# An attention and mixture-of-experts kernel: the transposition of each expert's next rows moved from TensorE to four DMA transposes

## The reference

```
xn    = x / rms(x) * norm_weight                 # 8192 x 512
idx   = top 512 tokens of each expert, by logit  # 16 x 512
h     = gelu(xn[idx] @ fc1[e].T + fc1_bias)      # 512 x 2048
y     = h @ fc2[e].T + fc2_bias                  # 512 x 512
out   = x + sum over experts of gate * y / sum of the token's chosen gates
```

## Time and profile before

| | us |
|---|---|
| median of 3 runs | 1980.07 (1979.4 to 1982.03) |
| the profiled execution | 1975.57 |
| its span in the trace | 1973.9 |
| TensorE matmul busy | 1897.5 (96%) |
| VectorE busy | 1493.6 (76%) |
| ScalarE busy | 1307.7 (66%) |
| GpSimd busy | 1224.7 (62%) |
| mean granted TensorE clock | 0.994 of full speed |

### The profile page before, as it was taken

How to read it: one execution, slowest core, us unless ns; L and a number is a source line. 1 busy time by engine, 2 the same in 40 slices (tenths; PEclk the granted TensorE clock), 3 DMA queues, 4 the chain that set the end, 5 groups by cost and what they waited for, 6 DMA issues and landing times.

```text
span 1973.9 us, 42032 instructions
## 1 busy us (share of the span) xinstructions
PE 1897.5 (96%) x12637; PEld 1693.8 (86%) x12637; DVE 1493.6 (76%) x2360; ACT 1307.7 (66%) x2594; POOL 1224.7 (62%) x1230
## 2 busy tenths in 40 slices
PE   4889999998889999999999999999999999999998
PEld 3678888877778899999998989899999999989897
DVE  5778878776887878777787777777787878778764
ACT  4667777763456666767677676767667676766664
POOL 3578888874056747566475756657574757657461
PEclk9999999999999999999999999999999999999999
DMA  7664444435743525254343534344352525335352
GB/s 283 219 193 151 120 132 135 120 87 182 238 107 114 148 94 154 86 152 107 125 121 122 142 104 135 101 138 127 113 153 87 155 86 154 107 128 133 112 123 44
DMA packets 90258, 263.19 MB, mean 133 GB/s; under 512 B 20593, under 2 KB 22353, under 8 KB 85073
## 3 DMA queue, kind: packets, MB, share of 16 engines
q1 hardware_dynamic: 70866, 211.44, 33.4%
q0 software_dynamic: 17024, 34.19, 8.9%
q10 hardware_dynamic: 2304, 16.78, 2.3%
HBM read 223.47 MB, written 55.60 MB: 141 GB/s over the span
## 4 chain that ended last, share of the span: by engine, by line
PE 71%; DVE 3%; issue 1%; POOL 0%; ACT 0%; DMA 0%; DVEq 0%; ACTq 0%; POOLq 0%
PE experts_b_a L2342 18%; PE experts_b_y L259 12%; PE experts_b_y L260 12%; PE experts_b_y L261 12%; PE experts_b_b L2342 9%; PE experts_b_c L2342 5%; PE experts_b_turn L2312 1%; PE experts_b_a L2442 1%; PE experts_b_c L2331 1%; PE experts_b_turn L2331 1%; DVE experts_y_out L2126 1%; DVE experts_x_lo L1987 0%; DVE experts_counts L2138 0%; DVE experts_hot_a L1911 0%; DMA experts_rows<-xn_dram,experts_ahead 0%
## 5 line engine op out<-in xcount | busy, mean ns | idle before, releaser
L1606 POOL TENSOR_TENSOR experts_s_raw<-experts_w_raw 128x256 f32<-128x256 f32 x128 | 156.4, 1222 | 406.7 <-DMA experts_w_raw<-in_w 392.3
L259 PE MATMUL experts_b_y<-experts_w_hi,experts_h_hi 128*128 128x512 f32 x1024 | 406.4, 397 | 1.2 <-DVE experts_h_lo L2065 1.2
L260 PE MATMUL experts_b_y<-experts_w_lo,experts_h_hi 128*128 128x512 f32 x1024 | 404.2, 395 | 0.0
L261 PE MATMUL experts_b_y<-experts_w_hi,experts_h_lo 128*128 128x512 f32 x1024 | 399.3, 390 | 0.0
L2342 PE MATMUL experts_b_a<-experts_x_hi,experts_w_hi 128*128 (+1 forms) x1024 | 288.5, 282 | 1.4 <-ACT experts_h L1814 0.7
L2342 PE MATMUL experts_b_a<-experts_x_hi,experts_w_lo 128*128 (+1 forms) x1024 | 289.6, 283 | 0.0
L2342 PE MATMUL experts_b_a<-experts_x_lo,experts_w_hi 128*128 (+1 forms) x1024 | 289.4, 283 | 0.0
L261 PEld LDWEIGHTS experts_b_y<-experts_w_hi,experts_h_lo 128*128 128x128 f32 x1024 | 192.4, 188 | 43.2
L259 PEld LDWEIGHTS experts_b_y<-experts_w_hi,experts_h_hi 128*128 128x128 f32 x1024 | 194.3, 190 | 25.6 <-DVE experts_h_lo L2065 1.6
L260 PEld LDWEIGHTS experts_b_y<-experts_w_lo,experts_h_hi 128*128 128x128 f32 x1024 | 194.3, 190 | 21.2
L2342 PEld LDWEIGHTS experts_b_a<-experts_x_hi,experts_w_hi 128*128 128x128 f32 x1024 | 194.2, 190 | 19.1 <-issue 1.4
(11 more groups left out here) (389 smaller groups left out, 5547.6 us busy)
## 6 DMA issues: line engine op xcount, KB each, us to landing
experts_w_raw<-in_w SPq DMA_DIRECT2D x256, 512.0 KB
bias<-in_bias SPq DMA_DIRECT2D x68, 256.0 KB, 4.1
spread_w<-weight_dram SPq DMA_DIRECT2D x32, 512.0 KB, 6.5
xn_dram<-wq_hi ACTq DMA_DIRECT2D x13, 1024.0 KB, 7.1
attend_q_x<-in_x SPq DMA_DIRECT2D x17, 256.0 KB, 2.8
attend_k_x<-in_x SPq DMA_DIRECT2D x17, 256.0 KB, 6.0
xn_dram<-rows_y_xn SPq DMA_DIRECT2D x17, 256.0 KB, 4.7
experts_b_sb<-in_b SPq DMA_DIRECT2D x16, 256.0 KB
```

What stands on the lines that cost most here:

```text
L259: nc.tensor.matmul(out, lh, rh, start=first, stop=False)
L260: nc.tensor.matmul(out, lh, rl, start=False, stop=False)
L261: return nc.tensor.matmul(out, ll, rh, start=False, stop=last)
L1606: nc.gpsimd.tensor_tensor(s1, a21, a22, ALU.add).then_inc(s_done, 1)
```

## The change

For the experts from the third on (n = 2 to 15, made ready in the 14 turns of the loop), the rows are transposed without TensorE. A float32 value is two 16-bit words. ScalarE copies `rows` into `x_raw` in two instructions, with the low words of a row before its high words (`part_rows`, at the ends of periods 1 and 2). SP waits for both and issues four DMA transposes of 16-bit words, each 128 partitions by 1024 words, from `x_raw` back into `rows` (`move_rows`, ahead of the weight load of its third turn). ScalarE then joins the two words of each value into `x_raw` with four instructions, each of 1024 words a partition (`x_join`), in the places of the former copies; the first waits for all four transposes. TensorE has no transposes and none of their waits in the loop. VectorE's sums read `x_raw` where they read PSUM. The gathers change places: gates at the start of an expert's loop, rows after the tenth chunk's sums of the expert before. `weigh` moves from the middle of period 2 to the end of period 7. The first turn (e = 0) is written out apart from the loop on SP and ScalarE and keeps the transposes on TensorE.

```diff
+                def move_rows(n):
+                    sp.wait_ge(rows_apart, (n - 1) * 2)
+                    alone(sp, passed)
+                    for i, c in enumerate((2, 3, 0, 1)):
+                        sp.dma_start_transpose(moved[:, :, i * P:(i + 1) * P],
+                                               rows_by_word[:, c, :, :].rearrange("p w d -> p (w d)")).then_inc(rows_moved, 16)
+
+                def of_expert(e):
                     for q in range(1, Q + 1):
+                        if q == 3 and not isinstance(e, int):
+                            move_rows(e + 1)
                         if q == 4:
                             load_b2(e)
...
                     alone(pool, passed)
-                        pool.wait_ge(x_turned, n * KD)
+                        if isinstance(n, int) and n == 1:
+                            pool.wait_ge(x_turned, KD)
+                        else:
+                            pool.wait_ge(x_raw_ready, (n - 1) * KD)
...
-                    fetch_rows(e + 1)
                     if first:
+                        fetch_rows(1)
                         weight_sums(2, 5, 1)
                         fetch_meta(1)
                         adopt(0)
+                    else:
+                        fetch_meta(e + 1)
...
                         elif q == 8:
-                            fetch_meta(e + 2)
+                            fetch_rows(e + 2)
...
+                def part_rows(n, a):
+                    half = slice(2 * a, 2 * a + 2)
+                    act.wait_ge(rows_in, n * CT * 16)
+                    nc.scalar.activation(rows_by_word[:, half, :, :], whole_rows[:, half, :, :], ACT.Copy).then_inc(rows_apart, 1)
+
+                def x_join(n, k):
+                    first = RAW_B12 if k < 2 else RAW_B22
+                    act.wait_ge(rows_moved, (n - 1) * CT * 16)
+                    nc.scalar.activation(raw_pairs[:, :, first:first + 2, k % 2, :],
+                                         moved.rearrange("p (w k) (b t) -> p w k b t", k=KD, b=2)[:, :, k, :, :], ACT.Copy)\
+                        .then_inc(x_raw_ready, 1)
...
+                        elif q in (4, 5):
+                            middle = (lambda: x_join(e + 1, (q - 4) * 2),)
+                            end = (lambda: x_join(e + 1, (q - 4) * 2 + 1),)
+                        elif not first and q in (1, 2):
+                            end = (lambda: part_rows(e + 1, q - 1),)
...
-                        elif q in (4, 5):
+                        elif not first and q == 6:
+                            after_c0 = lambda: make_list(e + 2)
+                        elif first and q in (4, 5):
                             after_c0 = lambda: turn_next(e + 1, (q - 4) * 2, e * Q + q)
```

More of the change, by code:

```diff
@@ L45 @@
 EP = E + 2
-CLEARED = 54
+CLEARED = 57
 ATTEND_SIGNALS = {
@@ L1584, in _ @@
                         load_w2(e * Q + (q + 2), q % 2)
+                of_expert(0)
+                with sp.Fori(1, E - 1) as e:
+                    of_expert(e)
                 last = E - 1
@@ L1868, in _, with of_expert @@
                        begin=(lambda: first_split(B22, x_raw[:, RAW_B22, :, :].rearrange("p k t -> p (k t)")), lambda: first_sum_split(T3, 6), lambda: first_sum_split(T4, 8)))
-                with act.Fori(0, E - 1) as e:
-                    side = act.snap((e + 1) % 2)
+                def of_expert(e, side):
+                    first = isinstance(e, int)
                     for q in range(1, Q):
                         middle, end = (), ()
[L1873 to L1878, removed]
+                        if first and q in (4, 5):
+                            middle = (lambda: x_copy(e + 1, (q - 4) * 2, b_c),)
+                            end = (lambda: x_copy(e + 1, (q - 4) * 2 + 1, b_turn),)
+                        elif q in (4, 5):
[3 more added lines that the diff above has]
+                            end = (lambda: part_rows(e + 1, q - 1),)
                         elif q == 6:
@@ L2278, in of_expert @@
                         elif q == 4:
-                            middle = (lambda: x_first(e + 1, 0, b_c),)
-                            end = (lambda: x_first(e + 1, 1, b_turn),)
+                            halves = [b_c[:, 0:HALF], b_turn[:, 0:HALF]] if first else [x_raw[:, RAW_B12, k, :] for k in range(2)]
+                            middle = (lambda: x_first(e + 1, 0, halves[0]),)
+                            end = (lambda: x_first(e + 1, 1, halves[1]),)
                             if first:
@@ L2283, in of_expert @@
                         elif q == 5:
-                            middle = (lambda: x_others(e + 1, 0, b_c),)
-                            end = (lambda: x_others(e + 1, 1, b_turn),)
+                            others = [(b[:, 0:HALF], b[:, HALF:CAP]) for b in (b_c, b_turn)] if first else\
+                                [(x_raw[:, RAW_B22, k, :], x_raw[:, RAW_B21, k, :]) for k in range(2)]
+                            middle = (lambda: x_others(e + 1, 0, *others[0]),)
+                            end = (lambda: x_others(e + 1, 1, *others[1]),)
                         elif q == 6:
@@ L2290, in of_expert @@
                             middle = (lambda: split_x_sums(e + 1, side),)
-                            if first:
-                                end = (lambda: weigh(1),)
+                            end = (lambda: weigh(e + 1),)
                         period(q, e * Q + q, middle=middle, end=end)
@@ L2529, in of_expert @@
                             after_p4 = lambda: turn_next(e + 1, (q - 4) * 2 + 1, e * Q + q)
-                        elif q == 6:
+                        elif first and q == 6:
                             after_c0 = lambda: list_after(e + 2)
```

29 lines of the change are left out of this document (20 added, 9 removed).

## The result

The changed kernel takes 1962.91 us (1957.91 to 1968.33, 5 runs), the one before 1980.45 (1979.4 to 1986.67, 5 runs) beside it: a ratio of 0.9908 [0.9887, 0.9928]. It is faster, by 18 us where 23 were forecast. The profiled execution took 1965.93 us (before 1975.57).

The account below looks back on a forecast made before the run. TensorE's own work was taken to bound the experts. 1975.57 - 24.9 + 1.5 = 1952.2 us for the profiled execution, plus 4.5 for the median, given as 1957; own range 1950 to 1965, wider range 1949 to 2005 at 0.80.

Parts of the forecast that it names:

- Periods 4 and 5: TensorE without transposes: each period falls from 11.44 to 10.55 us, in 14 experts, a gain of 24.9 us.
- ScalarE sorting: Each `part_rows`, after the last split of hidden values: 1.90 us, with ends 0.95 and 3.8; cost 0.
- ScalarE joining: Four copies at 1.05 us replace four of about 0.60; cost 0 if the transposes are there.
- VectorE's narrow place: Period 4, third sum before TensorE's seventh product: spare 0.2 us; loss 0 to 7 us, taken as 1.5.
- SP and the transposes: Issue fits a 4 us gap; landing taken as 9 us against a limit of 15.4 from issue; cost 0.
- GpSimd, "Cost 0": Exchanged gathers: row gathers 1.1 us longer, rows there with 4 us spare, sums 1 us later; cost 0.
- the price of `weigh`: VectorE, end of period 7: five steps under 1.04 us, where VectorE waited 1.02 us.
- The execution's own time: The profiled execution was forecast at 1952.2 us; the median of the runs 4.5 us above, given as 1957.
- 1 and 2: Transposes landing over 15.4 us after issue (0.13), or the queue handling eight blocks per DMA in series, 2369 us (0.11).
- rival 1: Transposes late: ScalarE stops in period 4, TensorE stands before its next period; 2062 us at 22.9 us landing; chance 0.13.
- Rival 4: Part lost at VectorE's narrow place or to 16-bit copies at twice the price: up to 1 us an expert, 1965 to 1976; 0.09.
- Rival 3: Gain given back: transposes take 16 to 18 us, or weights cause the same stall; 1976 to 1984 us; chance 0.07.

Follow-up runs that it names:

- e4_swap_apart: The kernel before with only the exchange of the gathers, and GpSimd's sums waiting for the second `h_lo`: 1977.67 us, ratio 0.9984.
- e1_apart: The changed kernel with GpSimd's four sums held back until VectorE's second `h_lo` of period 0 is done: 1950.74 us, ratio 0.9854.
- e5_turn4: `e1_apart` with the four transposes issued one turn later, at the start of SP's fourth turn: 1958.53 us, ratio 0.9885.
- e6_behind_w1: `e1_apart` with the transposes issued behind the first weight load of SP's fourth turn: 2088.29 us, ratio 1.054.
- after: The changed kernel as first measured, 1962.91 us, ratio 0.9908; its profiled execution took 1965.93 us.
- c_after: The changed kernel run again with no edit: 1962.31 us, ratio 0.9916 against the kernel before.
- e3_swap_only: The kernel before with the gathers exchanged, `weigh` moved and block sums waiting for added rows; TensorE still transposes: 1985.55 us, ratio 1.0042.

## Why the forecast held, and which terms failed

The main term was right by its mechanism. That the sum came within 6 us of the median (1962.9 for 1957) owes something to luck. Its terms add up to 1955.2 with no VectorE loss and to 1962.2 with the whole 7 us; the stated 1950 to 1965 was wider than that without a reason, and the loss that brought the time to its upper end isn't in the sum.

- **Periods 4 and 5, -24.9 us.** Right: 10.55 us each, the expert 85.70 for 87.47, 1.77 us, 14 times. Alone (from `e4_swap_apart` to `e1_apart`) it measures 26 us, with an interval of some 5 us to either side.
- **ScalarE sorting.** Chosen 1.90 us, measured 1.90. Cost 0 is right.
- **ScalarE joining.** Sized at 1.05, measured 1.37: four copies are 5.5 us and not 4.2, and VectorE's sums waited for them 4.5 us in all, 13 times. TensorE stays busy in these periods, so the mis-sizing costs nothing.
- **VectorE's narrow place, +1.5 us.** Nothing there: period 4 is 10.55 in experts where the forecast allowed up to half a microsecond more. The 1.5 us were put at the wrong place on the right engine.
- **SP and the transposes.** The issue takes 5.6 us, longer than the gap of 4 that was read off; the next weight load went at 1036.78, and no split waited for it on TensorE's path. Landing taken as 9 us, measured 7.0 to 7.9 (the join starts 7.5 to 8.7 us after the first issue where it waits, in `e5_turn4`). The limit was put at a join 5.16 us into period 4 (1046.9 less 1041.74); `e5_turn4` shows 5.1, though with a join of 1.37 us and not 1.05: the way from the weights' split to the last gelu was 3.1 us there, where 3.5 were read. "Beyond it every us costs 14" holds just beyond; for a join 7.55 us late the price is 9.5 an expert, a quarter more, for want of the clock in the forecast.
- **GpSimd, "Cost 0". This step failed, and the price of `weigh` with it.** It priced the gathers' lengths and landing, and not what GpSimd's next instructions meet. The sums behind the gather meet the last period's second `h_lo`. Before, with the gates' gather ahead of them, they met it lightly and at no cost; with the rows' gather there they cost 2.0 us in 4 or 5 experts of 15. In the profiled execution it is 10 us; `e1_apart` less the changed kernel gives 11.6 us of the medians. The forecast had seen that "VectorE's phase there depends on what GpSimd does beside it, which moves", and asked it of one place of one period. It priced `weigh` at under 1.04 us too, from its place before, where the five steps take 1.1. At the end of period 7 they take 2.2, beside GpSimd's sums, and VectorE's first sum of the next period starts 2.69 us into it and not 1.64. No run shows what this costs by itself; what follows from it is below. One of the five steps, before and after:

```profile
L1943 DVE TENSOR_TENSOR experts_chosen_sum<-experts_chosen_sum,experts_none_chosen 128x4 f32<-128x4 f32 x15 | 2.4, 163 | 0.5
...
L1988 DVE TENSOR_TENSOR experts_chosen_sum<-experts_chosen_sum,experts_none_chosen 128x4 f32<-128x4 f32 x15 | 9.4, 626 | 0.5
```

- **The execution's own time.** Forecast 1952.2, measured 1965.93: +10 for the five experts, and 6.8 us for the part ahead of the experts, which no edit touches: the first `p1_copy` came at 568.1 us and at 561.3 before, the latest and the earliest of the nine traces here; the other seven lie between 562.2 and 566.8. One and the same kernel has 568.1 and 562.7, so this part is the luck of the execution. In the other direction 1.5 us for the term that was nothing, and 1.3 for the one expert of before at 13.79 us. That gives 1952.2 + 10.1 + 6.8 - 1.5 - 1.3 = 1966.3.

The windows of the first 561 us, before and after, differ in the granted clock, 0.98 and 0.97, and by 38 matmuls done:

```profile
0.00:561.00 561.00, 497.41 (x3440) 433.73 (x3440) 423.42 (x897) 345.58 (x1018) 353.49 (x470) 0.98 0.53 168
```

and after:

```profile
0.00:561.00 561.00, 497.90 (x3402) 434.75 (x3402) 420.54 (x892) 341.98 (x1011) 352.05 (x470) 0.97 0.53 166
```

- **Rivals.** 1 and 2 fell: the landing is about half the limit, and the queue doesn't work block by block. One transpose of eight 128 x 128 blocks took 1.34 us of the queue; all 32 blocks landed in 7.0 us. The Trainium skill (VectorE: DVE Perf Modes, section The three transpose paths) has 1309 ns for one block; a row here has eight in about that time. `e5_turn4` and `e6_behind_w1` show that rival 1's mechanism is real, and begins where it was put. Rival 4 (1965 to 1976) is nearest to what happened in kind: part of the gain lost to VectorE, 0.7 us an expert on average, at a place that it doesn't name. Rival 3's stall from weights shows in one expert of `e1_apart`.

Two instructions that start 0.37 us apart mostly end in one of three ways (`h_lo` at 0.69, 1.05 or 3.06 us), and their starts, counted from the period's, differ by 10 to 20 ns. But the traces have one thing that goes with the outcome: the moment at which the DMA lands whose weights these sums read; GpSimd waits for it in front of them. The three traces with the exchange and without the added wait (`after`, `c_after`, `e3_swap_only`), experts 2 to 15, beside the kernel before:

```
                  landing, us from      h_lo, us       first sum, us    experts
                  h_lo's start
kernel before     -1.15 to -1.10      1.04 to 1.06     1.26 to 1.29       13
exchanged         -0.51 and -0.49     1.05, 1.06       1.27                2
                  -0.47 to -0.26      3.05, 3.06       0.74 to 0.76       14
                  -0.24 to  0.15         0.69          0.90 to 0.94       13
                   0.67 to  2.29         0.69          behind h_lo        10
```

(In three more, number 7 of each trace, the fourth gather comes so late that the sums stand behind `h_lo` too.) The exchanged kernels issue this load 0.5 us later in the period, behind VectorE's split of the weights, which the moved `weigh` holds up; and it lands 3.1 to 6.0 us after its issue, where it took 3.0 to 3.1, while the gather of rows (1 MB, the gates have 128 KB) lands beside it. So both moved parts can have their share in it. That the landing decides the outcome is an order seen in the 42 cases of the three traces; no run shows it as a cause, and why it should be one stays open.

The Trainium skill (SBUF — State Buffer, section Who interferes with whom) says that a VectorE instruction with two SBUF inputs contends with a GpSimd instruction that reads SBUF, and that the order of issue decides who blocks. The trace agrees with the first: `h_lo` and the sums are such instructions, and apart from each other they take 0.69 and 0.74 us. With the second it does not: `h_lo` started first and lost to three sums in a row.

## What to carry to other kernels

Before moving a DMA on an engine that shares work with another, list what stands behind it and what that will meet: here the length of the moved gather cost nothing, and the sums behind it 10 us. List too which transfers it will land beside. A few small operations can be twice as long at their new place (`weigh`, 1.1 and 2.2 us). If two such instructions must be near each other, order them with a semaphore, on the side that has time; here the wait cost nothing that shows and gave 11.6 us back. A part that is to be hidden has a limit that can be read from the timeline ahead of the change (5.16 us read, 5.1 measured), and past it the price depends on the length of the stall: joins up to 1.6 us late cost what they are late, and one 7.55 us late cost 9.5, as TensorE's clock fell.

## What the runs showed that was not expected

- Four SBUF-to-SBUF transposes of 16-bit words, 128 x 1024 each: 5.6 us of the queue and 7.0 us to the last packet (up to 7.9), in packets of 256 bytes. 1 MB in 7.0 us is 150 GB/s, with weight loads and gathers beside it. The Trainium skill (Advanced Engine Details and Errata, section X-Bar Transpose (TRN2)) has 350 to 400 GB/s; here the median issue of 1.34 us for each 256 KB allows no more than 196.
- ScalarE on 16-bit words with a stride: 2048 a partition in 1.90 us, as 2048 float32; 1024 in 1.37 us where 1024 float32 take 1.05. So the sorting goes by the count of elements, not of bytes; what makes the join dearer was not tried apart.
- After standing for 7.26 us TensorE worked at the lower clock level through the window of 5 us that follows (0.51), and lost about 2 us by it in each expert.
